# Feeding attention's operands with four DMA transfers in place of six, and one wait moved to the end of a stage

## The chip, the cores and the metric

The kernel runs on one core of a Trainium2 chip. The metric is the time of one execution on the device in microseconds; lower is better.

## The reference

The input x is 4 batches of 2048 tokens of 256 features. It is normalised per token to xn; the result is x plus attention of xn plus a routed feed-forward part of xn.

```python
q = (xn @ Wq.T + bq) * HEAD_DIM ** -0.5     # 16 heads of 16 features
k, v = xn @ Wk.T + bk, xn @ Wv.T + bv
out = softmax(q @ k.T) @ v                  # per batch and head, 2048 x 2048 scores
attn = out @ Wo.T + bo
# feed-forward: softmax gate, top 2 of 16 experts per token, each expert keeps its best
# 1024 tokens of a batch; gelu(xn @ w1 + b1) @ w2 + b2, summed; layer norm of xn + sum
```

All of it is in float32. With 4 batches and 16 heads there are 64 pairs of batch and head, called heads below.

## The kernel before

The work runs in four stages, `norm`, `project`, `attend` and `finish`, each a block that all engines enter and leave together; a block ends when the last engine has come to its end. Engines order themselves inside a block with semaphores; a transfer raises its semaphore by 16 when it has landed.

`norm` (to about 88 us) normalises the tokens, transposes them into `tok_all` and makes v.

`project` makes q and k. It goes over 16 blocks (`NBLK`) of 512 tokens, and in each over four chunks m (two halves of q's features, two of k's). TensorE multiplies into `qk_ps[m]` (L415); ScalarE copies the result twice, to `f32s` (L462) and rounded to `parts[m][:, 0]` (L464); GpSimd writes the remainder to `parts[m][:, 1]` (L479); SyncE stores both to `q_parts` or `k_parts` in DRAM (L489). There is one buffer `parts[m]` for each m, so ScalarE waits before L464 until the chunk's store of the block before has landed (`stored[m]`), and TensorE waits before it writes `qk_ps[m]` again until ScalarE has read it. From the seventh block on, TensorE puts matmuls of the first head's first pass between the chunks (`first_pass`, L427), 42 pieces in all, which VectorE reduces to maxima (L565, L570). The routing of the feed-forward part is computed on VectorE at the same time.

A head's scores use operands of three parts: for q the rows are high, low, high, and for k high, high, low, 16 rows each, so that one matmul over 48 rows adds up three products. A *feed* brings one head's 48 rows of 8 KB for q (`q_feat`) and 48 for k (`k_feat`) from DRAM, all 2048 tokens. Each head is fed twice: to the lower partitions (from 0, `LOWER`) for the first pass, which finds each row's maximum, and to the upper ones (from 64, `UPPER`) for the scores, where two more rows of q hold the negated maximum (`put_shift`, four small transfers from `turned`). There are two buffers of each. In `project`, SyncE issues three feeds between the stores: of head 0 (low), head 1 (low) and head 0 (up). TensorE waits for `fed_low` before a head's first first-pass piece, and for `fed_up` and `shift_in` before its first score.

`attend` goes over the 64 heads. In a head, TensorE goes over 16 key tiles; for each it makes five score matmuls (L858), two pieces (four matmuls) of the first pass of a later head (L848) and the weighing of v (L867); ScalarE makes the exponentials (L802), VectorE the maxima (L921). GpSimd uses its time for the expert search and splits halves of the tokens. SyncE issues, in a head g, in this order: the upper feed of head g+1 (once head g's first score is made), the store of att of head g-1, the shift rows of head g+1 (once VectorE has turned them), the lower feed of head g+3 (once head g+1's first pass is over), and, in turn, `put_split` or `put_moved`. `put_split` stores the staged half to `tok_hi_dram` and waits until that has landed before it loads x over it. The three waits for the parts to be stored (GpSimd before its memset of `v_head`, SyncE before its first feed, ScalarE at the second key tile) stand at the beginning of `attend`, because its buffers lie where `parts` was.

`finish` does the experts, the output projection and the last norm.

Of the kernel before, what the change touches and what calls it, by code (L numbers as in the profile page):

```python
# [23 lines left out]
F32 = mybir.dt.float32  # L24
# [6 lines left out]
ds = bass.ds  # L31
# [3 lines left out]
B, S, D = 4, 2048, 256  # L35
H = 16
HD = D // H
# [6 lines left out]
NBLK = TOKENS // BLK  # L44
BPS = S // BLK
ST = S // P
KC = D // P
# [5 lines left out]
FEAT = 3 * HD  # L53
# [5 lines left out]
HEAD_RING = 3  # L59
PAIRS = ST * 2  # L60
EARLY = 10
LOADS = 6
Q_ROWS, K_ROWS = (0, 1, 0), (0, 0, 1)
BEFORE = 6
HALVES = NBLK * KC

# [33 lines left out]
def build(nc, x, wqT, wkT, wvT, woT, bq, bk, bv, bo, wg, bg, w1, b1, w2, b2, gamma, beta, out):  # L100
    top = ExitStack()
    with top:
        def sb(name, shape, dt=F32, ctx=top):
            return ctx.enter_context(nc.sbuf_tensor(name, shape, dt))

        def ps(name, shape, ctx):
            return ctx.enter_context(nc.psum_tensor(name, shape, F32))

        def sem(name):
            return top.enter_context(nc.semaphore(name))  # L110


        q_parts = nc.dram_tensor("q_parts", [2, B * D, S], F32).ap()
        k_parts = nc.dram_tensor("k_parts", [2, B * D, S], F32).ap()
        att_dram = nc.dram_tensor("att_dram", [HEADS, P, BLK], F32).ap()
        mask_b = nc.dram_tensor("mask_b", [B * E, S], BF16).ap()
        xn_dram = nc.dram_tensor("xn_dram", [NBLK, P, TPB * D], F32).ap()
        moved_dram = nc.dram_tensor("moved_dram", [HALVES, P, BLK], F32).ap()
        tok_hi_dram = nc.dram_tensor("tok_hi_dram", [HALVES, P, BLK], F32).ap()
        inverse_dram = nc.dram_tensor("inverse_dram", [HEADS * BPS, PARTS, BLK], BF16).ap()  # L120

        passed = [sem(f"passed_{e}") for e in ("dve", "pe", "pool")]
        x_blocks = x.rearrange("(n t p) d -> n p t d", p=P, t=TPB)
        out_blocks = out.rearrange("(n t p) d -> n p t d", p=P, t=TPB)


        tok_all = sb("tok_all", [P, NBLK, KC * BLK])
        ident = sb("ident", [P, P])
        warm = sb("warm", [P, 1])
        minus_half = sb("minus_half", [P, TPB])  # L130
        att_out = sem("a_att_out")

        first = ExitStack()
        with first:
            v_all = sb("v_all", [P, B, H, ST, HD], ctx=first)
            route = sb("route", [B * E, S], ctx=first)
            power = sb("power", [B * E, TOP + 1], ctx=first)
            bits = sb("bits", [B * E, TOP + 1], I32, ctx=first)
            drops = sb("drops", [B * E, TOP + 1], I32, ctx=first)
            cand = sb("cand", [B * E, 1], I32, ctx=first)  # L140
            q_feat = [sb(f"q_feat{r}", [P, S], F32R, ctx=first) for r in range(2)]
            k_feat = [sb(f"k_feat{r}", [P, S], F32R, ctx=first) for r in range(2)]
            half_max = [sb(f"half_max{r}", [P, ST, 2], ctx=first) for r in range(HEAD_RING)]
            row_max = [sb(f"row_max{r}", [P, ST], ctx=first) for r in range(HEAD_RING)]
            shift = sb("shift", [P, SHIFT, ST], F32R, ctx=first)
            turned = sb("turned", [P, SHIFT * ST], ctx=first)
            fed_low = [sem(f"a_fed_low{r}") for r in range(2)]
            fed_up = [sem(f"a_fed_up{r}") for r in range(2)]
            piece, maxed, row_maxed = sem("a_piece"), sem("a_maxed"), sem("a_row_maxed")
            shift_rounded, shift_done = sem("a_shift_rounded"), sem("a_shift")  # L150
            shift_turned, shift_in = sem("a_shift_turned"), sem("a_shift_in")
            parts_stored = [sem(f"p_stored{m}") for m in range(2 * KC)]
            mid = ExitStack()
            with mid:
                wqT_sb = sb("wqT_sb", [P, KC, D], ctx=mid)
                wkT_sb = sb("wkT_sb", [P, KC, D], ctx=mid)
                bq_col = sb("bq_col", [P, KC], ctx=mid)
                bqs_col = sb("bqs_col", [P, KC], ctx=mid)
                bk_col = sb("bk_col", [P, KC], ctx=mid)
                logits = sb("logits", [P, TILES, E], ctx=mid)  # L160
                with ExitStack() as st:
                    norm(nc, sem, lambda *a: sb(*a, ctx=st), lambda *a: ps(*a, ctx=st), locals())
                banks = first.enter_context(ExitStack())
                m_ps = [ps(f"m_ps{r}", [P, 2 * BLK], banks) for r in range(2)]
                with ExitStack() as st:
                    project(nc, sem, lambda *a: sb(*a, ctx=st), lambda *a: ps(*a, ctx=st), locals())
            att = top.enter_context(nc.sbuf_tensor("att", [P, BLK], F32, side="right"))
            with ExitStack() as st:
                attend(nc, sem, lambda *a: sb(*a, ctx=st), lambda *a: ps(*a, ctx=st), locals())
        with ExitStack() as st:  # L170
            finish(nc, sem, lambda *a: sb(*a, ctx=st), lambda *a: ps(*a, ctx=st), locals())
# [199 lines left out]
def project(nc, sem, sb, ps, t):  # L371

    M = 2 * KC
# [4 lines left out]
    q_feat, k_feat, half_max, row_max, shift, turned = (t[w] for w in ("q_feat", "k_feat", "half_max", "row_max", "shift", "turned"))  # L378
# [10 lines left out]
    scored = sem("p_scored")  # L389
    rounded = sem("p_rounded")  # L390
    split = sem("p_split")
    stored = t["parts_stored"]
    shifted, exped = sem("p_shifted"), sem("p_exped")
    routed, route_t = sem("p_routed"), sem("p_route_t")
    chain = sem("p_chain")
# [7 lines left out]
    order = sb("order", [P, E])  # L403
# [4 lines left out]
    with nc.Block() as block:  # L408
# [75 lines left out]
        def _(sp):  # L484
# [5 lines left out]
                             parts[m][:, :, :].bitcast(F32)).then_inc(stored[m], 16)  # L490

            def feed(n, where, done):
                for dst, src, order in ((q_feat[n], t["q_parts"], Q_ROWS), (k_feat[n], t["k_parts"], K_ROWS)):
                    for j, part in enumerate(order):
                        sp.dma_start(dst[where + j * HD:where + (j + 1) * HD, :].bitcast(F32),
                                     src[part, n * HD:(n + 1) * HD, :]).then_inc(done[n], 16)

            def stores(lo, hi):
                with sp.Fori(lo, hi) as blk:
# [14 lines left out]
            rows = q_feat[0][UPPER + FEAT:UPPER + FEAT + SHIFT, :].bitcast(F32).rearrange("k (q j p) -> k q j p", j=quarters, q=ST)  # L514
            for j in range(quarters):
                sp.dma_start(rows[:, :, j, :], turned[j * SHIFT * ST:(j + 1) * SHIFT * ST, :]).then_inc(shift_in, 16)

        @block.vector
        def _(dve):
# [55 lines left out]
def attend(nc, sem, sb, ps, t):  # L575
# [13 lines left out]
    q_feat, k_feat, half_max, row_max, shift, turned = (t[w] for w in ("q_feat", "k_feat", "half_max", "row_max", "shift", "turned"))  # L589
# [9 lines left out]
    fed_low, fed_up, shift_in = t["fed_low"], t["fed_up"], t["shift_in"]  # L599
    piece, maxed, row_maxed = t["piece"], t["maxed"], t["row_maxed"]  # L600
    shift_rounded, shift_done, shift_turned = t["shift_rounded"], t["shift_done"], t["shift_turned"]
    parts_stored = t["parts_stored"]
    scored = sem("a_scored")
    exped = sem("a_exped")
    weighed = sem("a_weighed")
# [32 lines left out]
    def tile(g, kt):  # L638
        return g * ST + kt

    with nc.Block() as block:
        @block.gpsimd
        def _(pool):
            for done in parts_stored:
                pool.wait_ge(done, 16 * NBLK + 16)
            for r in range(R):
                pool.memset(v_head[r][:, :, :], 1.0).then_inc(ones_set, 1)
            pool.wait_ge(ones_set, R)
# [67 lines left out]
        @block.sync  # L716
        def _(sp):
            def feed(n, u, where, done):
                for dst, src, order in ((q_feat[u], t["q_parts"], Q_ROWS), (k_feat[u], t["k_parts"], K_ROWS)):
                    for j, part in enumerate(order):  # L720
                        sp.dma_start(dst[where + j * HD:where + (j + 1) * HD, :].bitcast(F32),
                                     src[part, ds(n * HD, HD), :]).then_inc(done[u], 16)

            def put_shift(n, u):
                rows = q_feat[u][SHIFT_ROWS, :].bitcast(F32).rearrange("k (q j p) -> k q j p", j=QUARTERS, q=ST)
# [18 lines left out]

            sp.sem_inc(att_out, 16)
            sp.sem_inc(prepared_out, 16)
            for done in parts_stored:
                sp.wait_ge(done, 16 * NBLK + 16)
            sp.wait_ge(piece, PAIRS)
            feed(2, 0, LOWER, fed_low)  # L750
            for dst, src in ((shift_bc[:, :], "beta"), (staged[:, 0:D].bitcast(F32), "bo")):
# [39 lines left out]
        def _(act):  # L791
            act.sem_inc(exped, R)  # L792
            act.sem_inc(att_read, 1)

            def exp(g, r, kt, j, first=False):
                if j == 0:
                    act.wait_ge(weighed, tile(g, kt) + 1)
                    if first and kt == 1:
                        for done in parts_stored:
                            act.wait_ge(done, 16 * NBLK + 16)  # L800
                act.wait_ge(scored, slot(g, kt, j) + 1)
                act.activation(prob[tile(r, kt) % R][:, cols(j)], s_ps[slot(r, kt, j) % R][:, wide(j)],  # L802
                               ACT.Exp).then_inc(exped, 1)
# [12 lines left out]
            def step(g, r, first=False, following=True):  # L816
                for kt in range(ST):
                    for j in range(NP):
                        exp(g, r, kt, j, first)
                        if following and (kt, j) == (ROUND_AT, 2):  # L820
                            round_shift(g + 1, r + 1)
                        if not first and (kt, j) == (LAG - 1, 2):
                            collect(g - 1)
# [625 lines left out]
```

## Time and profile before

| what | value |
|---|---|
| median of 3 runs | 3384.77 us (3381.11 to 3386.24) |
| the profiled execution | 3384.77 us, span 3383.0 us |
| busy: TensorE matmul, VectorE, ScalarE, GpSimd | 97%, 86%, 75%, 28% |
| transfers moved | 271.93 MB, mean 80 GB/s |
| feeds, q_feat and k_feat | 768 transfers of 128.0 KB, landing after 4.2 and 5.6 us (median) |
| first score matmul of `attend` | at 257.5 us |
| mean granted TensorE clock | 0.989 |

The span is the time from the first to the last instruction. Busy time of TensorE is not TensorE at its peak, since matmuls are pipelined. In rows, PE is TensorE, PEld its weight loads, DVE VectorE, ACT ScalarE, POOL GpSimd, SPq SyncE's queue of issued transfers.

### The profile page before, as it was taken

The page shows a single profiled execution, that of the slowest core. Times are in us where ns is not written, and L with a number is a line of the kernel's source. Part 1 is how long each engine was busy: PE and PEld are TensorE (multiplying, and loading weights), DVE is VectorE, ACT ScalarE, POOL GpSimd, SP SyncE. Part 2 cuts the span into 40 slices and gives each one's busy share as a digit, 9 for nine tenths or more (in the row PEclk, how much of TensorE's full clock was granted, in tenths as well). Part 3 has the DMA queues.
Part 4 walks back from the last instruction along what each step waited for, and adds up shares of the span by engine and source line. Part 5 has one row for each costly group of instructions (what it writes and reads, how often), then busy time and mean ns, then how long its engine had stood idle before and what let it go on. Part 6 is the DMA issues. An engine that isn't in the chain of part 4 may idle for free. (4 is left out here: it accounts for less than half of the span.)

```text
span 3383.0 us, 75004 instructions
## 1 busy us (share of the span) xinstructions
PE 3289.2 (97%) x20848; PEld 1702.7 (50%) x20848; DVE 2901.3 (86%) x2989; ACT 2524.3 (75%) x5724; POOL 933.5 (28%) x1340
## 2 busy tenths in 40 slices
PE   7999999999999999999999999999999999799998
PEld 6444444444444444444444444444444444488887
DVE  7758899999999999999999999999999998377777
ACT  3557788888888888888888888888888888544333
POOL 2550222222222222222222222222222222244443
PEclk9999999999999999999999999999999999899999
DMA  5783333333333333333333333333333332455554
GB/s 197 200 236 47 54 55 54 55 54 55 55 59 58 57 57 59 59 55 59 55 55 54 54 54 55 54 54 55 54 55 57 58 58 42 117 158 158 166 158 118
DMA packets 140694, 271.93 MB, mean 80 GB/s; under 512 B 30192, under 2 KB 76336, under 8 KB 128112
## 3 DMA queue, kind: packets, MB, share of 16 engines
q1 hardware_dynamic: 138144, 266.71, 37.4%
q8 instruction: 178, 2.92, 0.4%
q10 hardware_dynamic: 2256, 1.36, 0.2%
q14 instruction: 116, 0.95, 0.1%
HBM read 173.59 MB, written 84.93 MB: 76 GB/s over the span
## 5 line engine op out<-in xcount | busy, mean ns | idle before, releaser
L921 DVE TENSOR_REDUCE half_max<-m_ps 128x1 f32<-128x1024 f32 x2006 | 2363.5, 1220 | 223.9 <-PE m_ps L848 212.0
L802 ACT ACTIVATE prob<-s_ps 128x512 f32<-128x512 f32 (+1 forms) x5120 | 2191.1, 521 | 425.6 <-PE s_ps L858 417.0
L858 PE MATMUL s_ps<-q_feat,k_feat 50*128 50x512 f32 (+1 forms) x5120 | 1542.9, 397 | 13.8 <-ACTq L792 5.9
L848 PE MATMUL m_ps<-k_feat,q_feat 48*128 48x512 f32 x4012 | 1358.8, 444 | 20.3 <-DVE half_max L921 20.2
L858 PEld LDWEIGHTS s_ps<-q_feat,k_feat 50*128 50x128 f32 x5120 | 798.8, 185 | 994.7 <-ACT prob L802 880.9
L867 PE MATMUL a_ps<-prob,v_head 128*32 128x512 f32 x8192 | 1096.2, 607 | 0.0
L848 PEld LDWEIGHTS m_ps<-k_feat,q_feat 48*128 48x128 f32 x4012 | 599.0, 186 | 221.7 <-DVE half_max L921 211.3
L657 POOL TENSOR_TENSOR shift<-row_max,shift 128x16 fp32r<-128x16 f32 x63 | 14.0, 222 | 1164.1 <-ACT shift L809 1164.1
L867 PEld LDWEIGHTS a_ps<-prob,v_head 128*32 128x32 f32 x8192 | 161.4, 108 | 256.3 <-issue 217.8
L1221 ACT ACTIVATE g_hi<-g 128x512 fp32r<-128x512 f32 x128 | 81.0, 632 | 251.0 <-DVE g L1263 210.8
L1385 POOL TENSOR_TENSOR g_lo<-g,g_hi 128x512 fp32r<-128x512 f32 x128 | 173.5, 1355 | 224.3 <-ACT g_hi L1221 224.2
L683 POOL TENSOR_SCALAR step_of<-route,cand 64x256 f32<-64x256 f32 x217 | 198.5, 915 | 44.5 <-POOL held L684 38.3
L651 POOL COPY v_head<-v_all 128x256 f32 (+1 forms) x64 | 25.3, 397 | 667.2 <-PE a_ps L867 667.1
L684 POOL TENSOR_TENSOR held<-held,step_of 64x256 f32<-64x256 f32 x217 | 157.4, 726 | 39.8 <-POOL step_of L683 39.8
L1263 DVE TENSOR_TENSOR g<-g,mask_bc 128x512 f32<-128x512 f32 x128 | 133.7, 1044 | 33.3 <-ACT g L1218 20.8
L1155 PE MATMUL o_ps<-w_hi,g_hi 128*128 128x256 f32 x512 | 145.7, 284 | 9.3 <-POOL g_lo L1385 8.9
L1155 PE MATMUL o_ps<-w_lo,g_hi 128*128 128x256 f32 x512 | 144.9, 283 | 0.0
L1155 PE MATMUL o_ps<-w_hi,g_lo 128*128 128x256 f32 x512 | 143.7, 281 | 0.0
L1144 PE MATMUL h_ps<-xn_hi,w_hi 128*128 128x512 f32 x256 | 105.9, 414 | 11.9 <-DMA xn_lo<-tok_all 9.5
L479 POOL TENSOR_TENSOR parts<-f32s,parts 128x512 fp32r<-128x512 f32 x64 | 89.3, 1400 | 60.6 <-ACT parts L464 60.4
L1155 PEld LDWEIGHTS o_ps<-w_hi,g_hi 128*128 128x128 f32 x512 | 97.2, 190 | 17.1 <-issue 12.5
L1144 PE MATMUL h_ps<-xn_lo,w_hi 128*128 128x512 f32 x256 | 102.3, 400 | 0.0
(147 smaller groups left out, 2000.5 us busy)
## 6 DMA issues: line engine op xcount, KB each, us to landing
q_feat<-q_parts SPq DMA_DIRECT2D x384, 128.0 KB, 4.2
k_feat<-k_parts SPq DMA_DIRECT2D x384, 128.0 KB, 5.6
q_parts<-parts SPq DMA_DIRECT2D x32, 512.0 KB, 4.3
k_parts<-parts SPq DMA_DIRECT2D x32, 512.0 KB, 4.4
att_dram<-att SPq DMA_DIRECT2D x64, 256.0 KB, 6.3
mask_bc<-mask_b SPq DMA_DIRECT2D x128, 128.0 KB, 4.5
x_in<-in_x SPq DMA_DIRECT2D x16, 512.0 KB, 4.2
xn_dram<-xn SPq DMA_DIRECT2D x16, 512.0 KB, 4.8
```

What stands on the lines that cost most here:

```text
L479: pool.tensor_tensor(parts[m][:, 1, :], f32s[m % KC][:, :], parts[m][:, 0, :].bitcast(F32), ALU.subtract).then_inc(split, 1)
L683: do(pool.tensor_scalar(step_of[:, :], t["route"][:, c * PART:(c + 1) * PART], bound, None, ALU.is_ge))
L684: do(pool.tensor_tensor(held[:, :], held[:, :], step_of[:, :], ALU.add))
L802: act.activation(prob[tile(r, kt) % R][:, cols(j)], s_ps[slot(r, kt, j) % R][:, wide(j)], ACT.Exp).then_inc(exped, 1)
L848: ins = pe.matmul(m_ps[p % 2][:, k * BLK:(k + 1) * BLK], q_feat[r % 2][LOW, qt * P:(qt + 1) * P], k_feat[r % 2][LOW, key:key + BLK], start ...
L858: pe.matmul(s_ps[slot(r, kt, j) % R][:, wide(j)], k_feat[r % 2][UP, kt * P:(kt + 1) * P], q_feat[r % 2][UP, cols(j)], start=True, stop=Tru ...
L867: ins = pe.matmul(a_ps[qb * VW:(qb + 1) * VW, :], v_head[r % R][:, kt, :], prob[tile(r, kt) % R][:, qb * BLK:(qb + 1) * BLK], start=(kt == ...
L921: dve.tensor_reduce(half_max[r][:, p // 2, p % 2:p % 2 + 1], m_ps[p % 2][:, :], AX.X, ALU.max).then_inc(maxed, 1)
L1144: ins = pe.matmul(h_ps[e % 2][:, :], w, v, start=(c == 0 and k == 0), stop=(c == KC - 1 and k == 2))
L1155: ins = pe.matmul(o_ps[k], v, w[:, e, :], start=(e == 0 and m == 0), stop=False)
L1263: dve.tensor_tensor(g[e % 2][:, :], g[e % 2][:, :], mask_bc[q % 2][:, e % QTR, :], ALU.mult).then_inc(gated, 1)
L1385: pool.tensor_tensor(g_lo[e % 2][:, :], g[e % 2][:, :], g_hi[e % 2][:, :].bitcast(F32), ALU.subtract).then_inc(split, 1)
```

## The change

A feed is written as four transfers in place of six, in both stages. The rows of q's high and low part lie in two parts of the DRAM tensor; one transfer with the outer dimension 2 brings both (32 rows). For k the high part is read twice through a broadcast outer dimension of 2. The third block of 16 rows of each is brought as before, and now comes after both pairs. What lands where is the same. `LOADS`, the number of transfers that the waits count, goes from 6 to 4.

The waits for the stored parts are taken out of `attend` (GpSimd, SyncE, ScalarE). In their place SyncE waits for the same count at the end of `project`, behind the shift rows, so that the block ends for all engines only when the parts are stored.

```diff
-LOADS = 6
-Q_ROWS, K_ROWS = (0, 1, 0), (0, 0, 1)
+LOADS = 4
...
-            parts_stored = [sem(f"p_stored{m}") for m in range(2 * KC)]
...
-    stored = t["parts_stored"]
+    stored = [sem(f"p_stored{m}") for m in range(M)]
...
             def feed(n, where, done):
-                for dst, src, order in ((q_feat[n], t["q_parts"], Q_ROWS), (k_feat[n], t["k_parts"], K_ROWS)):
-                    for j, part in enumerate(order):
-                        sp.dma_start(dst[where + j * HD:where + (j + 1) * HD, :].bitcast(F32),
-                                     src[part, n * HD:(n + 1) * HD, :]).then_inc(done[n], 16)
+                q, k = (t[w][:, n * HD:(n + 1) * HD, :] for w in ("q_parts", "k_parts"))
+                pair, single = slice(where, where + 2 * HD), slice(where + 2 * HD, where + FEAT)
+                sp.dma_start(q_feat[n][pair, :].bitcast(F32), q).then_inc(done[n], 16)
+                sp.dma_start(k_feat[n][pair, :].bitcast(F32), k[0:1].broadcast_to([2, HD, S])).then_inc(done[n], 16)
+                sp.dma_start(q_feat[n][single, :].bitcast(F32), q[0:1].rearrange("k d s -> (k d) s")).then_inc(done[n], 16)
+                sp.dma_start(k_feat[n][single, :].bitcast(F32), k[1:2].rearrange("k d s -> (k d) s")).then_inc(done[n], 16)
...
+            for m in range(M):
+                sp.wait_ge(stored[m], 16 * NBLK + 16)
...
-            for done in parts_stored:
-                pool.wait_ge(done, 16 * NBLK + 16)
...
-            for done in parts_stored:
-                sp.wait_ge(done, 16 * NBLK + 16)
...
-            def exp(g, r, kt, j, first=False):
+            def exp(g, r, kt, j):
                 if j == 0:
                     act.wait_ge(weighed, tile(g, kt) + 1)
-                    if first and kt == 1:
-                        for done in parts_stored:
-                            act.wait_ge(done, 16 * NBLK + 16)
```

The `feed` of `attend` changes in the same way, with `ds(n * HD, HD)` for the head's rows.

## Rows read from the trace of the kernel before

**Rows 1.** The page, its parts 1, 3 (queues) and 6 (issues).

```profile
PE 3289.2 (97%) x20848; PEld 1702.7 (50%) x20848; DVE 2901.3 (86%) x2989; ACT 2524.3 (75%) x5724; POOL 933.5 (28%) x1340
...
q1 hardware_dynamic: 138144, 266.71, 37.4%
...
k_parts<-parts SPq DMA_DIRECT2D x32, 512.0 KB, 4.4
```

**Rows 2.** Waits, 257 to 2913 us: us in total, times, longest.

```profile
PEld s_ps L858 <- ACT prob L802: 880.0, 1060, 4.8
...
POOL shift_bc L675 <- DMA staged<-in_bo: 6.8, 1, 6.8
```

**Rows 3.** Waits of SyncE's queue, 257 to 2913 us.

```profile
SPq L728 <- DVE turned L912: 1769.0, 63, 34.4
```

**Rows 4.** Timeline of SyncE's issues, one head: start, duration, what.

```profile
1009.09 2.63 SPq L728 DMA_DIRECT2D q_feat<-turned  x4
1012.03 1.28 SPq L721 DMA_DIRECT2D q_feat<-q_parts  x3
...
1015.00 0.37 SPq L736 DMA_DIRECT2D tok_hi_dram<-staged  x1
...
1021.65 1.26 SPq L721 DMA_DIRECT2D q_feat<-q_parts  x3
...
1050.23 2.65 SPq L728 DMA_DIRECT2D q_feat<-turned  x4
```

**Rows 5.** Transfers, 1009 to 1012.7 us: the packets of four shift-row transfers.

```profile
DMA packets 136, 0.02 MB, mean 4 GB/s; under 512 B 136, under 2 KB 136, under 8 KB 136
```

**Rows 6.** Transfers, 258 to 258.5 us, a feed's start: packets, MB, share.

```profile
q1 hardware_dynamic: 14, 0.11, 59.4%
```

**Rows 7.** Transfers, 260 to 262.5 us, in the middle of feeds.

```profile
DMA packets 75, 0.30 MB, mean 121 GB/s; under 512 B 38, under 2 KB 38, under 8 KB 38
...
q1 hardware_dynamic: 75, 0.30, 100.5%
```

**Rows 8.** Timeline of SyncE's issues in project: a store, two feeds.

```profile
161.68 3.16 SPq L489 DMA_DIRECT2D k_parts<-parts  x2
165.05 1.62 SPq L495 DMA_DIRECT2D q_feat<-q_parts  x3
...
184.09 1.51 SPq L495 DMA_DIRECT2D q_feat<-q_parts  x3
```

**Rows 9.** Timeline of TensorE in project, idle time before it in brackets.

```profile
153.58 1.64 PE L427 MATMUL m_ps<-k_feat,q_feat 48*128 48x512 f32 x4 [2.69 <-DMA k_feat<-k_parts]
...
181.80 3.70 PE L415 MATMUL qk_ps<-tok_all,wqT_sb 128*128 128x512 f32 x8
```

**Rows 10.** Timeline of ScalarE in project.

```profile
149.07 0.69 ACT L464 ACTIVATE parts<-qk_ps,bk_col 128x512 fp32r<-128x512 f32 x1 [0.46 <-DMA k_parts<-parts]
...
154.68 0.69 ACT L464 ACTIVATE parts<-qk_ps,bqs_col 128x512 fp32r<-128x512 f32 x1 [4.35 <-DMA q_parts<-parts]
...
175.60 0.69 ACT L464 ACTIVATE parts<-qk_ps,bqs_col 128x512 fp32r<-128x512 f32 x1 [0.52 <-DMA q_parts<-parts]
```

**Rows 11.** Windows: length, PE, PEld, DVE, ACT, POOL busy (count), clock, DMA share, GB/s.

```profile
153.60:156.00 2.40, 2.40 (x5) 1.29 (x6) 1.59 (x2) 1.30 (x3) 0.56 (x1) 0.61 0.74 284
...
160.00:162.00 2.00, 2.00 (x5) 0.64 (x4) 0.00 (x0) 0.48 (x2) 1.26 (x1) 0.76 0.70 184
170.00:253.00 83.00, 79.87 (x203) 35.05 (x201) 42.45 (x38) 43.00 (x69) 43.41 (x35) 1.00 0.84 236
253.00:256.00 3.00, 0.00 (x0) 0.00 (x0) 0.17 (x2) 0.00 (x0) 0.00 (x0) 0.52 0.51 131
...
264.00:267.00 3.00, 3.00 (x15) 1.18 (x15) 1.24 (x2) 1.52 (x5) 0.62 (x1) 0.54 1.22 197
```

**Rows 12.** Timeline of SyncE's last issues in project.

```profile
249.91 2.08 SPq L489 DMA_DIRECT2D k_parts<-parts  x2
253.20 2.89 SPq L516 DMA_DIRECT2D q_feat<-turned  x4
```

More of the change, by code:

```diff
@@ L601, in attend @@
     shift_rounded, shift_done, shift_turned = t["shift_rounded"], t["shift_done"], t["shift_turned"]
-    parts_stored = t["parts_stored"]
     scored = sem("a_scored")
@@ L718, in feed @@
             def feed(n, u, where, done):
[L719 to L722, printed above, removed]
+                q, k = (t[w][:, ds(n * HD, HD), :] for w in ("q_parts", "k_parts"))
+                pair, single = slice(where, where + 2 * HD), slice(where + 2 * HD, where + FEAT)
+                sp.dma_start(q_feat[u][pair, :].bitcast(F32), q).then_inc(done[u], 16)
+                sp.dma_start(k_feat[u][pair, :].bitcast(F32), k[0:1].broadcast_to([2, HD, S])).then_inc(done[u], 16)
+                sp.dma_start(q_feat[u][single, :].bitcast(F32), q[0:1].rearrange("k d s -> (k d) s")).then_inc(done[u], 16)
+                sp.dma_start(k_feat[u][single, :].bitcast(F32), k[1:2].rearrange("k d s -> (k d) s")).then_inc(done[u], 16)
             def put_shift(n, u):
@@ L818, in step @@
                     for j in range(NP):
-                        exp(g, r, kt, j, first)
+                        exp(g, r, kt, j)
                         if following and (kt, j) == (ROUND_AT, 2):
```

## The prediction

> **What bounds the kernel now.** I read the page first. TensorE is busy for nearly all of the span, while the queue that carries SyncE's transfers takes 37% of the sixteen DMA engines' time [rows 1]. So nothing is gained by moving fewer or larger transfers unless some wait for one stands on the path. The table of waits for the attention stretch (257 to 2913 us) says whether it does. The reader is to see that its large entries are between engines (weight loads of the score matmuls on ScalarE's exponentials, 880 us), and that of its three entries for a transfer, all on GpSimd and each a single wait, the longest is 6.8 us [rows 2]; no matmul, exponential or maximum there waits for one. The queue's own waits come third: SyncE stands still for 1769 us in 63 waits before it issues the shift rows [rows 3], so an operand transfer has that much air. The one place where transfers decide is the project stage. There TensorE stands idle for 2.69 us until the first head's k_feat has landed at 153.58 us [rows 9], and ScalarE waits for its stores [rows 10]. From 170 to 253 us TensorE is busy for 79.87 of 83 us [rows 11], so what it loses at 153 us it does not get back before attention begins.
>
> **What the change does to one feed.** Before, a feed is six transfers of 16 rows of 8 KB, 96 rows. After, it is four: two of 32 rows, whose source has an outer dimension of 2 (two parts of q; for k a repeated row block), and two of 16 rows. Bytes and rows are the same. SyncE issues two fewer, which saves it 2 x 0.43 us (three take 1.28 us [rows 4]) of time of which it has 1769/63, 28 us, to spare per head; that is worth nothing.
>
> What decides is over how many DMA engines a transfer is spread. The trace has one transfer shaped like the new ones: the shift rows, with an outer dimension of 2 at the destination and 32 rows at the source. Four of them leave 136 packets [rows 5]. Four times 32 rows are 128; the other 8 are two small ones for each transfer. A transfer waits for sixteen counts, and I read two small packets as two engines that report. Those of today's feeds cover all sixteen engines: in 2.5 us of nothing but feeds and a bias load the queue takes 100.5% of them [rows 7]. So I take it that a transfer with an outer dimension of 2 runs on two engines, and that these are the same two each time.
>
> The Trainium skill says so outright (DMA: Bandwidth & Descriptors, on why a DMA increments its semaphore by 16, and in the rules for kernel authors): the engines used are the largest number up to 16 that divides the slowest dimension of both sides, and a leading broadcast of c copies confines the whole DMA to c engines. By that rule the pairs get two engines; the trace's 136 packets agree.
>
> **How long two engines take.** Each gets 16 rows of q and 16 of k, so 32 packets of 8 KB in series. A lone 8 KB packet takes 0.34 us (14 packets in 59.4% of 16 x 0.5 us, 4.75 us [rows 6]). Crowded, with sixteen engines writing into the same 16 partitions, it is 1.06 us (100.5% of 16 x 2.5 us is 40.2 us; less some 0.9 us for 38 small ones, over 37 [rows 7]). I take 0.34 to 0.45 us, near the lone value, because after the change only two engines work at a time. The pairs then need 10.9 to 14.4 us, where a whole feed now takes about 6.
>
> **In attention it is hidden.** A head takes 41.1 us (1009.09 to 1050.23 [rows 4]). Its two feeds put 64 rows on each of the two engines, 21.8 us at 0.34, plus some 3 us for their share of the rest: 25 of 41 us. Follow the queue in a head that also stores a split half. The lower feed begins at 1012.03; the two engines are free again at about 1024 to 1027 instead of 1018. The store of tok_hi issued at 1015.00 stands behind it on those two engines, so SyncE, which waits for that store before it goes on, issues the upper feed not at 1021.65 but at about 1026 to 1029, and it lands at about 1038 to 1045. Next are the shift rows at 1050.23, which the score matmuls need within some 6 us: they meet an empty queue. The att store goes 15 us later too, but is needed a head later. The lower feed has over 30 us. I cost all this at 0; its cover is the gap of 21 us before 1050.23.
>
> **In the project stage it is not.** Term 1: the first feed. The store ahead of it lands at 149.07 [rows 10], so its rows start at about 148. Now the last lands just before 153.58. After: 148 + 32 x 0.34 to 0.45, plus about 1.4 us for two single rows among sixteen engines, is 160.3 to 163.8; I take 160.2, which is 6.7 us later. The stores issued behind it wait on the same two engines and are late by the same, not more. Bounds: from 147.5 with one lone single row, 159.1, 5.5 us later; at 0.6 us a packet (halfway to the crowded value) 169, 16 us later. The clock comes on top. Granted TensorE clock is at its half level (1.2 GHz) from 154 to about 161 us after those 2.7 idle us, and again from 253 to nearly 267 after 6 idle us [rows 11, 12]: some 6.8 and 9.3 us of running. An idle stretch of 9 us should look like the second, and cost (9.3 - 6.8)/2 = 1.3 us more. Term 1 is 8.0 us.
>
> Terms 2 and 3: the feeds at 165.05 and 184.09 us [rows 8]. The two engines first finish the stores issued at 161.68 (until about 167.5), then come 10.9 us of pairs and 1 us of single rows, and then the next store, for which I count 2.3 of its usual 4.4 us to landing [rows 1]: it lands at about 181.7, where ScalarE went on at 175.60 [rows 10]. It is 6.1 us late. TensorE's next matmul into that bank is at 181.80, 5.5 us after that activation ended [rows 9, 10]: it loses 0.6 us. Two such feeds are 1.2 us; from 0 (they are absorbed) to 6 us each, if a packet beside stores takes 0.5 us or the half clock returns.
>
> Term 4: the waits for the stored parts go from GpSimd, ScalarE and SyncE in attention to SyncE at the stage's end, where every engine meets. The last stores are issued by 252.0 and land 4.4 us later by the median [rows 1], at 256.4; SyncE is busy with the shift rows until 256.09 [rows 12]. Nobody waits for more than 0.3 us. If the stores were late by the 6 us of term 2, all of that would show here; that is in the range.
>
> Sum: 8.0 + 1.2 + 0.3 = 9.5 us. The profiled execution took 3384.77 us (span 3383.0), which is also the median, so 3394.3 us.
>
> **Rivals.** The first, not slower: the pairs are spread over all sixteen engines, or the lateness is absorbed. For it speaks that I know the splitting from a 4 KB transfer alone. Then 32 rows reach twice the partitions at once, and the first feed lands up to 2 us earlier with two issues fewer: 3382.5 to 3391 us.
>
> The Trainium skill has two rules behind this (SBUF — State Buffer, on the DMA port swizzle, and the rule below its size curve): 32 partitions reach 8 ports where 16 reach 4, 189 against 104 GB/s, and transfers should be coalesced. Today's feeds run at 121 GB/s or so, in agreement with the first figure; by these rules the feed would halve and the time fall by some 3 us.
>
> The second, much slower: the two engines become the bound in attention. It decides from 0.60 us a packet, (41.1 - 3)/64. Each 0.1 us beyond costs 64 x 0.1 x 62 heads = 397 us; at the crowded 1.06 us it is some 1800 us, 5200 in all. For it speaks the crowded row, against it that the crowd is gone. The sign of it would be TensorE waiting for q_feat or k_feat at the start of each head.
>
> The third, faster: all waits for transfers in the project stage go, because fourteen engines are left to the stores. Bound: 2.69 us of idle and half of 6.8 us at the half clock, -6.1 us, plus some of ScalarE's 4.4: down to 3376 us. The stores use the slow two engines as well, which speaks against it.
>
> **Chances.** My forecast 0.62, the first rival 0.22, the second 0.10, the third 0.06. Here 0.2% is 6.8 us, about what a measurement of this kernel tells from no change. Of the forecast's own range, 3389 to 3406, about a fifth lies within it. So slower is 0.50 + 0.10 = 0.60, same 0.12 + 0.22 = 0.34, faster 0.06. The range 3383 to 3412 leaves out the second rival, the third and the forecast's upper tail.
>
> **What would show it.** The landing time of k_feat's transfers some 5 to 10 us longer; TensorE's first m_ps matmul at about 160 instead of 153.58; ScalarE's waits for stores in the project stage longer than the 4.35 us that is now the longest [rows 10]; attention beginning some 9 us later; the head still 41.1 us long. The forecast is wrong if a feed leaves as many small packets as today, or if heads grow.

## The result and the profile after

The changed kernel takes 3404.18 us (median of 4 runs, 3402.16 to 3411.43) where the kernel before, on the same chip, takes 3382.94 us (4 runs). The ratio, taken over 20 runs of the changed kernel, is 1.0068, with a 95% interval of 1.0056 to 1.0081: slower by 0.68%, some 23 us by that ratio and 21 by the medians. Forecast were 3394.3 us and 9.5 us more; the direction and the mechanism came, the size is off by a factor of more than two. The profiled execution took 3403.66 us, span 3401.9.

First the page of the changed kernel: busy time, packets, queue, and three rows of its issues.

```profile
PE 3291.1 (97%) x20848; PEld 1704.6 (50%) x20848; DVE 2901.9 (85%) x2989; ACT 2523.9 (74%) x5724; POOL 933.2 (27%) x1340
...
DMA packets 133014, 271.90 MB, mean 80 GB/s; under 512 B 22512, under 2 KB 68656, under 8 KB 120432
...
q1 hardware_dynamic: 130464, 266.68, 27.2%
...
k_parts<-parts SPq DMA_DIRECT2D x32, 512.0 KB, 4.6
...
att_dram<-att SPq DMA_DIRECT2D x64, 256.0 KB, 14.2
```

No engine has more work than before. The bytes are the same, but the queue has 7680 packets fewer than in [rows 1] (138144 less 130464). That number says over how many engines the pairs run: 768 feed transfers with 16 small packets each were 12288; 256 pairs with 2 and 256 single ones with 16 are 4608; the difference is 7680 exactly. The store of att, 128 partitions wide, now lands after 14.2 us (6.3 before): its share on two of the engines stands behind an upper feed.

Next the transfers of the changed kernel from 156 to 158 us, when only the first feed's pairs are left.

```profile
DMA packets 12, 0.10 MB, mean 49 GB/s; under 512 B 0, under 2 KB 0, under 8 KB 0
...
q1 hardware_dynamic: 12, 0.10, 11.7%
```

Twelve packets start in 2 us and take 11.7% of 16 x 2 us, 3.74 us: two engines, busy nearly without a gap, at 0.312 us a packet. That is a little under the 0.34 us of [rows 6], and what sixteen crowded engines took, 1.06 us, does not come back.

The timeline of TensorE in project, where [rows 9] had 153.58 us for the first of these rows:

```profile
159.85 2.07 PE L425 MATMUL m_ps<-k_feat,q_feat 48*128 48x512 f32 x4 [7.04 <-DMA k_feat<-k_parts]
161.85 5.93 PE L413 MATMUL qk_ps<-tok_all,wkT_sb 128*128 128x512 f32 x8
...
186.73 1.19 PE L425 MATMUL m_ps<-k_feat,q_feat 48*128 48x512 f32 x4
189.47 5.40 PE L413 MATMUL qk_ps<-tok_all,wqT_sb 128*128 128x512 f32 x8 [1.55 <-ACT parts L462]
194.80 1.19 PE L425 MATMUL m_ps<-k_feat,q_feat 48*128 48x512 f32 x4
...
213.54 5.40 PE L413 MATMUL qk_ps<-tok_all,wqT_sb 128*128 128x512 f32 x8 [1.71 <-ACT parts L462]
```

ScalarE's timeline, which answers to [rows 10], has the cause of the second and the third stall:

```profile
160.96 0.69 ACT L462 ACTIVATE parts<-qk_ps,bqs_col 128x512 fp32r<-128x512 f32 x1 [9.07 <-DMA q_parts<-parts]
...
188.74 0.69 ACT L462 ACTIVATE parts<-qk_ps,bqs_col 128x512 fp32r<-128x512 f32 x1 [7.60 <-DMA q_parts<-parts]
...
212.80 0.69 ACT L462 ACTIVATE parts<-qk_ps,bqs_col 128x512 fp32r<-128x512 f32 x1 [9.34 <-DMA q_parts<-parts]
```

And the windows of the changed kernel, columns as in [rows 11]:

```profile
156.00:159.80 3.80, 0.00 (x0) 0.00 (x0) 0.00 (x0) 0.00 (x0) 0.00 (x0) 0.52 0.12 48
...
162.00:167.00 5.00, 5.00 (x7) 2.12 (x8) 1.46 (x2) 2.15 (x4) 2.23 (x2) 0.56 0.67 202
...
190.00:194.00 4.00, 4.00 (x7) 1.69 (x6) 0.00 (x0) 3.72 (x6) 3.86 (x4) 0.57 0.57 174
```

From 156 to 159.8 us no engine computes at all and DMA is busy for 12%: fourteen of the sixteen engines have nothing to do while two work off the pairs. Later, 1.55 us of idle time at 188 us is followed by a mean granted clock of 0.57 in the 4 us from 190, that is 3.4 us at the half level, so eight matmuls take 5.40 us where they otherwise take 3.70. Behind the third feed the same happens once more: 1.71 us of idle time at 212 us, and 5.40 us for eight matmuls.

Where the profiled executions part, by the start of the same instruction in each: first m_ps matmul 6.3 us later, the one at 194.80 us (185.43 before) 9.4, the first score matmul 12.7 (270.18 against 257.50), head 3 11.3, head 62 11.0, head 63 13.8, the last stage's first matmul 16.9, the end 18.9 us. Between head 3 and head 62, 59 heads, the difference changes by 0.3 us in all. These are differences between single profiles. The first score matmul is at 254.44 us in e1 and at 255.51 in e4, whose project stages have six-transfer feeds like the kernel before, and between 269.1 and 272.5 us in all seven profiles with narrow pairs throughout project (the changed kernel, e2, e5, e8, e9, e10, e12). So the shift of attention's start is clear, but its size is 12.7 us only against this one profile.

What is left is in two places that the forecast did not have. In head 62 ScalarE stops for 4.35 us that no semaphore accounts for:

```profile
2849.11 1.15 ACT L798 ACTIVATE prob<-s_ps 128x256 f32<-128x256 f32 x3 [0.42 <-PE s_ps L854]
2854.61 1.64 ACT L798 ACTIVATE prob<-s_ps 128x512 f32<-128x512 f32 x4 [4.35 <-issue]
```

At that place the kernel before stands for 1.90 us. The trace has a fetch of 8 KB on another queue (q14, "instruction") that is through 1.2 to 1.3 us before ScalarE goes on. It starts 11.46 us after the head's first exponential in the kernel before and 13.72 us after it in this one, when the head's upper feed is nearly through (its last packet starts at 15.0 us). The other place is the end of attention, in SyncE's timeline:

```profile
2930.05 0.33 SPq L733 DMA_DIRECT2D att_dram<-att  x1
2933.69 0.40 SPq L1073 DMA_DIRECT2D w_raw<-in_w  x1
```

Before, these two are 0.74 us apart (2916.31, 2917.05), now 3.64. One more such fetch runs in the gap, 1.73 us after its start, and a second starts 0.30 us behind it; before, there is none. All engines wait for SyncE at the block's end.

### The profile page after: what moved, and what is told of

Read it like the earlier page. It is cut to its first block and busy times, and to the rows that moved or that the text cites. A ratio compares the mean times of both kernels' runs of the same rounds, so it can differ in the third digit from the quotient of the medians.

```text
span 3401.9 us, 74505 instructions
## 1 busy us (share of the span) xinstructions
PE 3291.1 (97%) x20848; PEld 1704.6 (50%) x20848; DVE 2901.9 (85%) x2989; ACT 2523.9 (74%) x5724; POOL 933.2 (27%) x1340
## 3 DMA queue, kind: packets, MB, share of 16 engines
q1 hardware_dynamic: 130464, 266.68, 27.2%
## 5 line engine op out<-in xcount | busy, mean ns | idle before, releaser
L1140 PE MATMUL h_ps<-xn_hi,w_hi 128*128 128x512 f32 x256 | 105.9, 414 | 15.5 <-DMA xn_lo<-tok_all 12.7
## 6 DMA issues: line engine op xcount, KB each, us to landing
att_dram<-att SPq DMA_DIRECT2D x64, 256.0 KB, 14.2
```

The costliest lines, as they stand in the source:

```text
L1140: ins = pe.matmul(h_ps[e % 2][:, :], w, v, start=(c == 0 and k == 0), stop=(c == KC - 1 and k == 2))
```

## The experiments

Each kernel is compared with runs of the kernel before on its own chip.

**e1, only the wait moved** (six transfers a feed):

```diff
             for j in range(quarters):
                 sp.dma_start(rows[:, :, j, :], ...).then_inc(shift_in, 16)
+            for m in range(M):
+                sp.wait_ge(stored[m], 16 * NBLK + 16)
```

with the three waits in `attend` taken out.

> Six-transfer feeds as before; only the waits for the stored parts move to the end of project. My theory (the loss is the pairs' confinement to two DMA engines): the last stores have landed within 0.3 us of SyncE's shift rows, so attention begins at 257.5 to 257.8 us and the time is that of before, 3383 us, plus or minus 3. A rival, that moving the wait and the shift of all later instructions in the program cost time: 3 to 8 us more, with the gap before the last stage's first weight load 3 us longer, as in the changed kernel.

3381.2 us against 3381.52, ratio 1.0006 (0.9996 to 1.0015). The moved wait costs nothing that can be measured, and the trace says why: the last store has landed at 252.41 us, and SyncE issues the shift rows until 253.02. Attention begins at 254.44 us, 3 us before the place that was named; TensorE waits 0.75 us for the first feed in this profile, where the kernel before has 2.69.

**e2, only the feeds**: the change's `feed` in both stages, the waits where they were.

> Four-transfer feeds with the pairs; the waits for the stored parts stay at the beginning of attention. My theory: nearly all of the loss is here. The first feed has landed at about 160 us, TensorE waits 7 us for it, attention begins at about 269 to 270, time 3400 to 3404 us. The rival that the moved waits cost: 3390 or less.

3404.51 us, ratio 1.0074 (1.0060 to 1.0088). The whole loss is in the feeds. TensorE waits 6.9 us for the first one. The time is just above the range named, and attention begins at 272.50 us, 2.5 us later than was expected.

**e3, the pairs interleaved and wide**:

```diff
-                sp.dma_start(q_feat[n][pair, :].bitcast(F32), q)
-                sp.dma_start(k_feat[n][pair, :].bitcast(F32), k[0:1].broadcast_to([2, HD, S]))
+                sp.dma_start(q_feat[n][pair, :].bitcast(F32), q.rearrange("k d s -> d k s"))
+                sp.dma_start(k_feat[n][pair, :].bitcast(F32), k[0].unsqueeze(1).broadcast_to([HD, 2, S]))
```

in both feeds. The sum over the rows does not depend on their order, as long as q and k have the same.

> The changed kernel with the pairs' rows interleaved (feature by feature, the two parts beside each other) so that the outer dimension of both sides is a multiple of 16. Same bytes, same number of transfers, same moved waits. My theory: a pair leaves sixteen small packets in place of two, the first feed lands at or before 153.6 us, ScalarE's waits of 8 to 9 us for stores are gone, time 3380 to 3386 us. A rival, that fewer and larger transfers are what makes the feed late (or that two rows of 8 KB from two parts of the tensor are slow to read): the loss stays, above 3395 us.

3386.54 us, ratio 1.0015 (1.0006 to 1.0024). The page of this kernel, packets and the landing of the pairs:

```profile
DMA packets 136598, 271.92 MB, mean 80 GB/s; under 512 B 26096, under 2 KB 72240, under 8 KB 124016
...
k_feat<-k_parts SPq DMA_DIRECT2D x128, 256.0 KB, 4.9
```

4096 small packets fewer than before are 256 transfers fewer of sixteen each, so every pair now has sixteen. TensorE waits 1.01 us for the first feed, which lands at 155.3 us and so not by the 153.6 that was named; no wait of ScalarE for a store is longer than 2.7 us. As many and as large transfers as in the change, and four fifths of its loss are gone: it was their spread. The time ends just above the range named; what is left is the subject of e6.

**e4, the pairs in attention alone**: project's `feed` is that of before with six transfers, and the waits count them.

> The changed kernel with project's three feeds in six transfers; the pairs only in attention. My theory: the 12.7 us of project are gone and attention begins at 257.5 to 258; what is left is a late fetch of instructions behind an upper feed in the last heads (2.75 us) and what the layout of the program brings: 3386 to 3391 us. A rival, that attention pays too, head by head: above 3395 us, with heads longer than 41.2 us.

3391.18 us, ratio 1.0031 (1.0019 to 1.0042); the first score matmul is at 255.5 us, where 257.5 to 258 were named. The time is just above the range. In its profile head 62 has the same gap of 4.97 us between exponentials (from the start of one to the start of the next; 4.37 us of it idle), the end of attention loses 2.8 us, and 6 us more go between heads 0 and 3. There the granted clock is at its half level in spells whose length differs from profile to profile; I do not know what sets them. They are not the pairs' doing: e6, below, has no narrow pair and the same 51.2 us at the half level between 249 and 368 us (the kernel before has 30.8), and it loses 4.7 us there. Both profiled executions are also among the longest of their kernels.

**e5, the pairs in project alone**: the converse.

> The converse of e4: project's three feeds with the pairs, attention's in six transfers, waits moved. My theory: TensorE waits 7 us for the first feed, attention begins 12 to 13 us later than before, ScalarE's stall in the last heads but one is 2.5 us as before and not 5.0: 3391 to 3396 us. If attention carried a share that only shows together with project, this would be under 3388.

3395.72 us, ratio 1.0035 (1.0022 to 1.0048), at the upper end of the range. In its profile attention begins 13.2 us later than before, and ScalarE's gap in head 62, measured as in e4, is 2.41 us. e4 and e5 together are 1.0066, the change 1.0068: within their intervals, each some 0.0012 to either side, the two stages add up.

**e11, only the first feed narrow** (e5, with project's second and third feeds interleaved and wide):

```diff
+                narrow = (n, where) == (0, LOWER)
-                sp.dma_start(q_feat[n][pair, :].bitcast(F32), q)
+                sp.dma_start(q_feat[n][pair, :].bitcast(F32), q if narrow else q.rearrange("k d s -> d k s"))
```

and the same for k.

> Project's first feed with the narrow pairs of the change, its second and third with interleaved wide ones, attention's feeds in six transfers, waits moved. It parts the 12.7 us that project lost. If the first feed's landing is worth its 6.3 us and the other two the 6.4 us that are left (by the changed kernel's timeline, 3.3 each), attention begins 6 to 7 us later than before, at 264 us, and the time is 3387 to 3391 us. If the whole loss followed from the first feed (its lateness pushes the later two into a worse place), attention begins at 268 us or later.

3390.5 us, ratio 1.0021 (1.0011 to 1.0031). Two rows of its TensorE timeline:

```profile
160.53 2.07 PE L427 MATMUL m_ps<-k_feat,q_feat 48*128 48x512 f32 x4 [9.12 <-DMA k_feat<-k_parts]
...
264.71 0.76 PE L857 MATMUL s_ps<-q_feat,k_feat 50*128 50x512 f32 x1 [5.81 <-ACTq L793]
```

Attention begins 7.2 us later than in the profile of the kernel before and not 13 (9 to 10 us later than in e4 and e1). The second and third feed cost the rest: 5.5 us against the changed kernel's profile and 6.0 against e5's. They are not a consequence of the first.

**e12, the last two upper feeds wide**: the changed kernel, with the interleaved pairs only where the head's number is past the loop.

> The changed kernel with only the upper feeds of the last two heads interleaved and wide. My theory of ScalarE's stall of 4.35 us in the last head but one: a fetch of its instructions runs on one of the DMA engines that the narrow pair fills, and waits behind it. Then that gap between exponentials falls from 4.97 to about 2.4 us, as in all kernels with sprayed feeds, and the fetch comes 2.5 us earlier. If the place in the program is what matters, the gap stays at 4.97 us, since the instructions are as many as in the changed kernel.

One run, 3400.69 us. ScalarE's timeline at the place of the 4.35 us:

```profile
2850.52 1.15 ACT L800 ACTIVATE prob<-s_ps 128x256 f32<-128x256 f32 x3 [0.42 <-PE s_ps L856]
2853.58 3.30 ACT L800 ACTIVATE prob<-s_ps 128x512 f32<-128x512 f32 x7 [1.91 <-PE s_ps L856]
```

The gap between exponentials is 2.52 us again, the fetch comes 11.45 us after the head's first exponential and not 13.72. In all the kernels whose upper feed is sprayed in that head (before, e1, e3, e5, e6, e7, e11, e12) the gap is 2.3 to 2.5 us, in those whose feed is narrow (after, e2, e4, e9, e10) 4.9 to 5.0. The one kernel that breaks the row confirms the reading: in e8, further down, the feed is narrow too, but its last packet starts 14.69 us after the head's first score and the fetch only at 15.81, and the gap is 2.4 us. So the fetch stands behind the narrow pair when it comes while that is under way. That it is ScalarE's, and that it runs on one of the same two engines, is what fits; the trace names neither the owner nor a packet's engine.

What it costs depends on the profile it is held against. Head 62 is 47.7 us long in the changed kernel and 45.0 in the kernel before, but 42.3 to 42.5 us in e1, e3, e5, e6, e7, e11 and e12. The kernel before is the only one with a sprayed feed whose clock falls in that head; here are its window and e12's, columns as in [rows 11]:

```profile
2827.60:2872.60 45.00, 43.31 (x257) 18.80 (x253) 35.09 (x31) 35.17 (x82) 3.88 (x3) 0.92 0.17 36
```

```profile
2840.00:2882.50 42.50, 40.80 (x256) 17.73 (x253) 35.02 (x31) 34.75 (x82) 3.73 (x3) 1.00 0.17 39
```

So the narrow feed costs this head 2.7 us against the one profile of the kernel before and 5.2 us against e12, about half of it the longer gap and the rest the clock (0.93 in the changed kernel's head). Whether the kernel before usually has that spell is not known.

**e6, e3 with 24 waits added** that are always met, behind SyncE's loop:

```diff
+            for _pad in range(24):
+                sp.wait_ge(piece, PAIRS)
             sp.wait_ge(v_ready, (B - 1) * H)
```

> e3 (interleaved, wide pairs) with 24 waits that are always met added to SyncE's program behind its loop in attention. My theory of e3's remaining 5 us (and of 3 of the changed kernel's 21): SyncE's shorter program puts a fetch of instructions between its last store of att and the end of the block, where all engines wait 2.9 us for it; the added instructions move that fetch to a place where SyncE waits anyway. Then SyncE's drain follows that store within 0.5 us and the time is about 3 us less than e3's, 3383 to 3384 us. A rival, that the last stage is slower for another reason: no change against e3.

3383.84 us, ratio 1.0001 (0.9993 to 1.0010), where e3 has 1.0015. SyncE's timeline at the end of attention, e3 first and then e6:

```profile
2911.05 0.33 SPq L733 DMA_DIRECT2D att_dram<-att  x1
2914.70 0.41 SPq L1073 DMA_DIRECT2D w_raw<-in_w  x1
```

```profile
2918.25 0.33 SPq L733 DMA_DIRECT2D att_dram<-att  x1
2919.00 0.40 SPq L1075 DMA_DIRECT2D w_raw<-in_w  x1
```

The gap of 3.65 us is 0.75 again, with more instructions than before it. It was the place at which SyncE's changed program has to fetch, and nothing that the transfers do. The other kernels agree: the gap is 0.74 to 0.76 us and without a fetch in before, e1, e5, e6, e7, e9, e10 and e11, and 3.6 to 3.8 us with one in the changed kernel, e2, e3, e4, e8 and e12. A longer program is no cure by itself: e8 adds more transfers than e10 and has the gap, e10 does not. In time, the intervals of e3 and e6 still overlap by a little.

**e9, the changed kernel with the same 24 waits.**

> The changed kernel itself with the 24 always met waits in SyncE's program behind its loop in attention, as in e6. If 3 us of the change's 21 are a fetch of SyncE's instructions at the end of attention, SyncE's drain follows its last store within 0.5 us again and the time is 3 us less than the changed kernel's, 3400 to 3402 us. If the pairs account for all of it, 3404 us or more.

3403.07 us, ratio 1.0057 (1.0044 to 1.0071); its gap is 0.76 us as well. The ratio is lower than the change's by 0.0011, some 4 us, but the intervals overlap, and the medians differ from the kernel before by 18.9 and 21.2 us. The time lies between the two that were named. The gap's closing is shown, its 2.9 us in the time are not separated from the scatter; e3 and e6 lean the same way. In this profile heads 3 to 62 take 1.3 us more than in the changed kernel and head 62 takes 0.9 more, for no reason that I know, so that its end is only 0.6 us earlier.

**e7, the kernel before with the first feed issued a block earlier**:

```diff
-            stores(0, BPS + 1)
+            stores(0, BPS)
             for m in range(M):
                 sp.wait_ge(stored[m], 16 * BPS + 16)
             feed(0, LOWER, fed_low)
-            stores(BPS + 1, BPS + 3)
+            stores(BPS, BPS + 3)
```

> The kernel before, with the first feed issued one block of stores earlier. My theory that the first feed's landing is on the path and nothing after it gives time back: TensorE no longer waits 2.7 us at 151 us, its clock does not fall there, attention begins 4 to 6 us earlier, 3376 to 3378 us. A rival, that project is paced by its stores, or that the stores held up behind SyncE's earlier wait cost as much: within 2 us of before.

3385.08 us, ratio 1.0008 (1.0000 to 1.0017). I was wrong here. TensorE's timeline has the wait gone and another in its place:

```profile
150.79 5.15 PE L415 MATMUL qk_ps<-tok_all,wqT_sb 128*128 128x512 f32 x8 [4.34 <-ACT parts L464]
155.87 1.19 PE L427 MATMUL m_ps<-k_feat,q_feat 48*128 48x512 f32 x4
```

The feed goes out at 140.18 us, the stores behind it are late, ScalarE waits 8.7 us for one and TensorE 4.34 us for ScalarE. The DMA engines are full in this stretch (a share of 1.07 from 148 to 151 us in the kernel before), so an earlier feed only changes who waits. The landing of the first feed is on the path when it comes later, not when it comes earlier.

**e8 and e10, more load on the two engines**: the changed kernel with five and with two transfers per head of the pairs' source shape, from `q_parts` to a spare tensor, behind the lower feed.

```diff
                     feed(g + 3, (r + 3) % 2, LOWER, fed_low)
+                    for c in range(5):
+                        sp.dma_start(t["spare_dram"][ds(g * 5 + c, 1)].rearrange("n k d s -> (n k) d s"),
+                                     t["q_parts"][:, ds((g + 3) * HD, HD), :]).then_inc(copied, 16)
```

> The changed kernel with five more transfers per head of the pair's source shape (outer dimension 2, 256 KB each) from q_parts to a spare tensor in DRAM, behind the lower feed. They put 80 more packets of 8 KB on each of the two engines: 144 x 0.312 us and 3 us make 48 us of a head's 41.2. My theory, that these transfers share two engines of a fixed rate: heads of 48 us or more, so at least 400 us more, 3800 us or above, with TensorE waiting for operands. If the copies spread over other engines or the two had more room than counted, the time stays under 3450 us.

4067.64 us, one run. The copies did not go out as expected, 8 KB at a time: the trace has four packets of 64 KB for each, two on each engine, of 2.4 us. That is 0.30 us for 8 KB, so the load is the one that was counted, 47 us a head. Heads are 52 us long, and among the waits from 1000 to 2700 us TensorE has a new one, 7.9 us a head:

```profile
PE s_ps L860 <- DMA q_feat<-turned: 257.3, 32, 11.5
```

> As e8, with two copies per head instead of five: 96 packets of 8 KB a head on each of the two engines, 96 x 0.312 us and 3 us are 33 us of 41.2. My theory, a fixed rate of two engines with a point from which it decides: the head stays 41.2 us long and the time stays within 10 us of the changed kernel, 3400 to 3414 us. If instead every packet in front of the shift rows or the stores cost something, two fifths of e8's loss would show, 270 us.

3422.06 us, one run, 18 us above the changed kernel and out of the range. The waits from 300 to 2900 us say by what:

```profile
PE s_ps L860 <- DMA q_feat<-turned: 14.1, 16, 1.7
```

The two engines have room for two copies, but SyncE issues in order. In the timeline of e10 the store of tok_hi goes out at 1035.14 us, and SyncE gets past its landing only at 1056.38; the upper feed goes out at 1056.98, 11.7 us ahead of the next shift rows at 1068.67 (elsewhere 10.7). Its pairs alone take 10 us on the two engines, and the store of att follows them, so the shift rows stand behind both. So two things decide in attention, the rate (five copies) and before it the order in the queue (two); the order has a part in e8 too, whose heads are longer than the rate alone asks for and where the mean granted clock falls to 0.87. In the changed kernel itself the same wait has grown from 6.07 us (1015.00 to 1021.07) to 13.66, as its timeline shows, and is still covered:

```profile
1020.31 2.68 SPq L729 DMA_DIRECT2D q_feat<-turned  x4
...
1026.00 0.38 SPq L737 DMA_DIRECT2D tok_hi_dram<-staged  x1
1039.66 0.41 SPq L739 DMA_DIRECT2D staged<-in_x  x1
1040.26 0.67 SPq L720 DMA_DIRECT2D q_feat<-q_parts  x1
...
1043.51 0.38 SPq L733 DMA_DIRECT2D att_dram<-att  x1
```

## Why the prediction was right, and where it was not

**Two engines** (right). The reading from the 136 packets of the shift rows held for all 256 pairs, to the packet. e3 shows that the spread is the cause: one change of the order of the dimensions and most of the loss is gone. The Trainium skill's rule (DMA: Bandwidth & Descriptors, rules for kernel authors), that the outermost dimension of both sides should be a multiple of 16, agrees with e3's sixteen packets a pair.

**0.34 to 0.45 us a packet** (a little high). It was 0.312 us, and the first feed came 6.3 us late where I had taken 6.7. Two numbers there do not follow from their own terms: the 160.2 us that I took lies just under the 160.3 of the sum, and at 0.6 us a packet the sum is 168.6 us, 15 us later and not 16.

**Term 1, 8.0 us** (the step held, its clock part did not). e11 has 7.2 us for the first feed with its consequences, against the profile of the kernel before. The clock fell as forecast, for 10.2 us from 156.1, but part of that lay in the idle stretch; TensorE ran 6.4 us at the half level, no more than the 6.8 before.

**Terms 2 and 3, 1.2 us in all** (the step that was mis-sized). The timeline gives 3.1 us from the first feed to 194.80 us and 3.3 more to attention, e11 5.5 to 6.0 us by undoing both. The lateness was close: ScalarE went on at 188.74 us, 7.1 us behind where the kernel before would have been with the first 6.07 us taken off, against a forecast of 6.1. But TensorE's air was only 5.5 us, so one more microsecond there was one more of idle, 1.55 us instead of 0.6, and that idle stretch was followed by the half clock, 1.7 us on one block of matmuls. The third feed repeats it with 1.71 and 1.7 us. I had put both into the bounds (0 to 6 us each) and not into the sum.

**Term 4, 0.3 us** (right). In the changed kernel the last store has landed at 268.25 us and SyncE is done with the shift rows at 268.78, so nobody waits; e1 agrees.

**Attention at 0** (right for 59 heads, wrong for one). The queue went as followed: the upper feed goes out 19.95 us after the shift rows (1020.31 to 1040.26), where I had 17 to 20. But I had followed only the transfers that SyncE issues. Fetches of instructions stand in no queue of the program; one of them, in the unrolled heads behind the loop, met a narrow feed and cost 2.75 us against the one profile of the kernel before, and 5.2 against e12.

**Not in the forecast at all**: 2.9 us at the end of attention from where SyncE's program has to fetch, and some 2 us in the last stage. That stage is 459.5 to 460.6 us long in all the profiles with four-transfer feeds in attention and in e5, 459.1 in e11, and 457.9 to 458.4 in the kernel before, e1 and e7. e3 and e6, where every pair is sprayed, have it too, so the spread is not its cause, which stays open. With these the profiled executions come to 18.9 us: 12.7 + 2.75 + 2.9 + 2, less 1.4 in the first heads, where one spell of half clock is 6.8 us long and not 13.7.

**The range** held the result in part by luck. Its upper end rested on packets of 0.6 us, which did not come; some 8 of the 21 us are from places that the forecast did not have.

**The rivals.** That the pairs spread over sixteen engines is refuted by the packets. The rules of the Trainium skill on ports and on coalescing (SBUF — State Buffer, on the DMA port swizzle and below the size curve) would, as I read them, have halved a feed; the 121 GB/s of [rows 7] also agree with its 104 only roughly. Even e3, with 32 partitions over sixteen engines, lands k's pair after 4.9 us and its last single after 5.6, and in the kernel before k's transfers landed after 5.6. A whole upper feed takes 7.6 us in e3 from its first issue to its last landing and 8.1 in the kernel before, a lower one 8.7 and 9.4 (medians). No gain from it reached the time. The second rival, a bound in attention, needs 0.60 us a packet or more load; e8 has it. The third did not come.

## What to carry to other kernels

Before merging transfers, look at the outermost dimension on both sides: the count of small packets that one such transfer leaves in the trace tells how many engines it uses, and a pair of blocks as the outer dimension makes it two. Put the long dimension outside and the pair inside. And where a queue's share of the DMA engines falls while its transfers land later, as here from 37.4% to 27.2%, the transfers have become narrow, not cheap.

## What the runs showed of the hardware that I had not expected

A fetch of instructions can stand behind the kernel's own transfers. An 8 KB fetch behind a narrow feed came 2.3 us later, and the engine's gap went from 2.4 us to between 4.9 and 5.0, in five kernels; in e8, where the fetch came after the feed, it stayed at 2.4. A program whose instructions lie a little differently can be 2.9 us slower at the end of a block: SyncE's gap there was 0.74 to 0.76 us in eight kernels, among them e1, e6, e9 and the kernel before, and 3.6 us or a little more in six, among them the changed kernel and e3. And each of two engines moves 8 KB rows at a steady 0.312 us, while sixteen engines at work on [rows 7] took 1.06 us each: eight times the engines gave between two and three times the rate (121 against 49 GB/s). That the shared partitions are the reason is not shown.
